# A selective-scan block on one core: projections in neighbouring slots, C products in the other two of four, one read per job

## What is computed

```python
xz = h @ in_w                       # xs and z, 512 channels each
xs = silu(xs)
proj = xs @ xproj_w                 # dt (512), B (64), C (64)
dt = softplus(proj[..., :512] + dt_bias)
A = -exp(A_log)
# at each time step, for 512 channels x 64 states:
hst = hst * exp(dt_t[:, :, None] * A) + (dt_t * x_t)[:, :, None] * B_t[:, None, :]
y_t = einsum('bds,bs->bd', hst, C_t)
# after the scan
y = (ys + xs * Dskip) * silu(z) @ out_w
```

## Time and profile before

| | us |
|---|---|
| median of 3 runs (5270.68 to 5274.25) | 5272.7 |
| the profiled execution's own time | 5272.58 |
| its span | 5270.9 |
| PE busy | 4869.9 (92%) |
| DVE busy | 4721.3 (90%) |
| POOL busy | 3754.7 (71%) |
| ACT busy | 3384.6 (64%) |
| DVE scans (L894), 2048 of them | 4536.0 |

### The profile page before, as it was taken

How to read it: one execution, slowest core, us unless ns; L and a number is a source line. 1 busy time by engine, 2 the same in 40 slices (tenths; PEclk the granted TensorE clock), 3 DMA queues, 4 the chain that set the end, 5 groups by cost and what they waited for, 6 DMA issues and landing times. The chain is left out here.

```text
span 5270.9 us, 130492 instructions
## 1 busy us (share of the span) xinstructions
PE 4869.9 (92%) x44784; PEld 2658.3 (50%) x44784; DVE 4721.3 (90%) x2419; ACT 3384.6 (64%) x11498; POOL 3754.7 (71%) x6613
## 2 busy tenths in 40 slices
PE   6999999999999999999999999999999999776898
PEld 4555555555555555555555555555555555443444
DVE  2999999999999999999999999999999999996443
ACT  4767767676766766676766767676676767663112
POOL 4787878777787878777787878687887878674211
PEclk8999999999999999999999999999999999998999
DMA  3121211112121211112121211111121211113442
GB/s 107 39 65 45 65 38 54 56 39 62 43 61 44 66 41 50 56 40 62 43 61 43 67 40 52 55 45 56 43 61 43 64 40 46 31 29 111 145 153 68
DMA packets 433144, 306.75 MB, mean 58 GB/s; under 512 B 215920, under 2 KB 336240, under 8 KB 432496
## 3 DMA queue, kind: packets, MB, share of 16 engines
q1 hardware_dynamic: 428272, 294.39, 18.7%
q10 hardware_dynamic: 4224, 4.19, 0.2%
HBM read 187.27 MB, written 111.15 MB: 57 GB/s over the span
## 5 line engine op out<-in xcount | busy, mean ns | idle before, releaser
L894 DVE TENSOR_TENSOR_SCAN b_hs<-b_dA,b_u 128x1024 f32<-128x1024 f32 x2048 | 4536.0, 2270 | 184.5 <-ACT b_u L821 155.5
L1057 PE MATMUL b_ex<-b_dd,b_aw 32*128 32x512 f32 x8192 | 2751.5, 641 | 17.6 <-POOL b_dd L542 15.6
L1044 PE MATMUL b_u<-b_ud,b_bw 32*128 32x256 f32 x16384 | 2320.1, 400 | 276.9 <-DVE b_hs L894 255.9
L803 ACT ACTIVATE b_dA<-b_ex 128x496 f32<-128x496 f32 x4096 | 2303.5, 593 | 166.0 <-PE b_ex L1057 127.5
L1044 PEld LDWEIGHTS b_u<-b_ud,b_bw 32*128 32x128 f32 x16384 | 1417.5, 184 | 1122.7 <-issue 558.1
L821 ACT ACTIVATE b_u<-b_hin 128x32 f32<-128x32 f32 x1792 | 368.8, 206 | 1236.8 <-PE b_u L1044 1045.4
L542 POOL TENSOR_TENSOR b_dd<-b_dr,b_mask 128x512 f32<-128x512 f32 x1024 | 1074.9, 1050 | 51.5 <-DVE b_hs L894 39.8
L1076 PE MATMUL b_y<-b_hs,b_cw 128*32 128x256 f32 x16384 | 1104.8, 385 | 1.7 <-DVE b_hs L894 1.7
L551 POOL TENSOR_TENSOR b_ud<-b_ur,b_mask 128x512 f32<-128x512 f32 x1024 | 1085.6, 1060 | 0.0
L1057 PEld LDWEIGHTS b_ex<-b_dd,b_aw 32*128 32x128 f32 x8192 | 865.4, 183 | 62.0 <-ACT b_dA L803 35.7
L1076 PEld LDWEIGHTS b_y<-b_hs,b_cw 128*32 128x32 f32 x16384 | 426.9, 108 | 846.2 <-issue 663.3
(11 more groups left out here) (104 smaller groups left out, 2351.0 us busy)
## 6 DMA issues: line engine op xcount, KB each, us to landing
b_u<-scratch_ut SPq DMA_DIRECT2D x256, 128.0 KB, 2.9
scratch_y<-b_ysb SPq DMA_DIRECT2D x128, 256.0 KB, 2.1
scratch_xs<-b_xs SPq DMA_DIRECT2D x64, 256.0 KB, 2.5
scratch_sz<-b_sd SPq DMA_DIRECT2D x64, 256.0 KB, 2.2
scratch_dt<-b_sd SPq DMA_DIRECT2D x64, 256.0 KB, 2.1
scratch_ut<-b_uT SPq DMA_DIRECT2D x64, 256.0 KB, 2.6
b_ur<-scratch_ut SPq DMA_DIRECT2D x1024, 16.0 KB
b_dr<-scratch_dt SPq DMA_DIRECT2D x1024, 16.0 KB, 1.7
```

What stands on the lines that cost most here:

```text
L803: nc.scalar.activation(dA[:, j % NDA, h, :, 1:TC], src[:, :, 1:TC], ACT.Exp).then_inc(exp_done, 1)
L894: nc.vector.tensor_tensor_scan(hs[:, v, :, :, kp].rearrange("p d t -> p (d t)"), dA[:, j % NDA, :, :, :].rearrange("p h d t -> p (h d t)") ...
L1044: ins = nc.tensor.matmul(dst[:, :, tb, :], bw[row(r), c % 2, tb, :], ud[row(r), j // 2 % NPR, tb, :, :], start=(tb == 0), stop=(tb == NTB ...
L1057: nc.tensor.matmul(e[bank_of[what]][:, :], aw[row(r), p % DIRS, v, :, :].rearrange("p b s -> p (b s)"), dd[row(r), (p * PAIRS + j // 2) % ...
```

## The change

Four things move at once.

1. On PE, of every four slots the first two may have a piece of a job and the last two a C pair (before: pieces in even slots, C pairs in odd ones). The two pieces of a job, or two XZ jobs, stand in neighbouring slots. Most jobs begin a few slots earlier.
2. ACT reads a job once. `take_xz` copies; a new `bend` makes the tanh of both halves from SBUF. `take_dt` adds the bias; Abs and Relu follow from SBUF in `log_part`. The side work on ACT is two generators: `readers` is stepped between the two halves of `decay`, `works` at the slot's end, where `unit` was.
3. `share_banks` guesses anew when a holder is read: first the half 0, then the job, then the half 1.
4. `log_part` begins two slots earlier against POOL; POOL's `times_sigmoid` come one slot later for the first five, and the last three move to other slots.

```diff
-        XZ_SLOT = ((0, 2), (4, 6), (8, 10), (12, 14), (16, 18), (86, 88), (98, 100), (104, 106))
-        DT_SLOT, DT_SPAN = (22, 38, 54, 70), 3
-        BC_SLOT, BC_SPAN = (32, 48), 3
-        UT_SLOT, UT_SPAN = (64, 80, 82, 96), (2, 2, 1, 1)
-        BT_SLOT = 66
+        XZ_SLOT = ((0, 1), (4, 5), (8, 9), (12, 13), (16, 17), (84, 85), (92, 93), (100, 101))
+        DT_SLOT, DT_SPAN = (20, 36, 52, 68), 2
+        BC_SLOT, BC_SPAN = (28, 44), 2
+        UT_SLOT = (60, 76, 80, 96)
+        BT_SLOT = 61
...
-                        give(("e", 2 * (slot + 2) + h), slot + 0.9 + 0.25 * h)
+                        give(("e", 2 * (slot + 2) + h), slot + 0.9 + 0.5 * h)
...
-                        give(("job", n), slot + slots + 0.2)
+                        give(("job", n), slot + slots + 0.1)
...
+                    pool.wait_ge(relued, m + 1)
                     nc.gpsimd.tensor_tensor(sd[:, j, :], pre[:, m % 2, :], ln[:, :], ALU.add).then_inc(dt_made, 1)
...
+                    yield
                     for i in range(JB + 1):
                         yield
                         times_sigmoid(q, i)
                         yield from wait_steps(3)
-                    yield from wait_steps(9)
+                    yield from wait_steps(8)
...
                         sum_dt(q, j)
-                        yield from wait_steps(4)
+                        yield from wait_steps(2)
+                        if j + 1 == JB:
+                            times_sigmoid(q, JB + 1)
+                        yield from wait_steps(2)
                         times_x(q, j)
-                        yield from wait_steps(4 if j + 1 < JB else 2)
-                    times_sigmoid(q, JB + 1)
-                    yield from wait_steps(7)
+                        if j + 1 < JB:
+                            yield from wait_steps(4)
+                    yield from wait_steps(5)
                     times_sigmoid(q, JB + 2)
-                    yield from wait_steps(6)
+                    yield from wait_steps(8)
                     times_sigmoid(q, JB + 3)
...
-                    nc.scalar.activation(dst[:, cols], job_bank(n)[:, 0:SEQ], ACT.Copy, scale=0.5)
+                    nc.scalar.activation(dst[:, b * SEQ:(b + 1) * SEQ], job_bank(n)[:, 0:SEQ], ACT.Copy, scale=0.5
+                                         ).then_inc(freed, 1)
+
+                def bend(q, i):
+                    m = q * SILUS + i
+                    src = xs[:, i, :] if i < JB else sd[:, i - JB, :]
+                    act.wait_ge(freed, first_job(q) + XZ_JOB[i] + CB)
                     if m >= 2:
                         act.wait_ge(silu_made, m - 1)
-                    nc.scalar.activation(th[:, i % 2, cols], job_bank(n)[:, 0:SEQ], ACT.Tanh, scale=0.5).then_inc(freed, 1)
+                    nc.scalar.activation(th[:, i % 2, :], src, ACT.Tanh).then_inc(bent_up, 1)
...
+                    nc.scalar.activation(pre[:, m % 2, b * SEQ:(b + 1) * SEQ], job_bank(n)[:, 0:SEQ], ACT.Identity,
+                                         bias=dtb[:, q % DIRS, j:j + 1]).then_inc(freed, 1)
+
+                def log_part(q, j):
+
+                    m = q * JB + j
+                    act.wait_ge(freed, first_job(q) + DT_JOB[j] + CB)
                     if m:
                         act.wait_ge(nd_made, 2 * m)
-                    if m >= 2:
-                        act.wait_ge(dt_made, m - 1)
-                    nc.scalar.activation(pre[:, m % 2, cols], job_bank(n)[:, 0:SEQ], ACT.Relu, bias=bias)
-                    nc.scalar.activation(ey[:, cols], job_bank(n)[:, 0:SEQ], ACT.Abs, bias=bias).then_inc(freed, 1)
...
+                    nc.scalar.activation(ey[:, :], pre[:, m % 2, :], ACT.Abs).then_inc(bent, 1)
+                    yield
+                    act.wait_ge(bent, 3 * m + 1)
                     nc.scalar.activation(ey[:, :], ey[:, :], ACT.Exp, scale=-1.0).then_inc(bent, 1)
...
                     nc.scalar.activation(wy[:, :], wy[:, :], ACT.Identity, bias=less[:, :]).then_inc(logged, 1)
+                    yield
+                    nc.scalar.activation(pre[:, m % 2, :], pre[:, m % 2, :], ACT.Relu).then_inc(relued, 1)
...
+                def works(q):
+
+                    nc.scalar.preload_act_table_set("exp_and_others")
+                    yield from wait_steps(2)
+                    for i in range(JB + 1):
+                        bend(q, i)
+                        yield
+                        plus_one(q, i)
+                        yield from wait_steps(3)
+                    nc.scalar.preload_act_table_set("natural_log_exp_and_others")
+                    yield from wait_steps(4)
+                    for j in range(JB):
+                        yield from log_part(q, j)
...
+                    nc.scalar.preload_act_table_set("exp_and_others")
+                    yield from wait_steps(4)
+                    for i in range(JB + 1, SILUS):
+                        bend(q, i)
+                        yield
+                        plus_one(q, i)
+                        yield from wait_steps(7)
...
-                        if j + 2 < JP:
-                            decay(p, j + 2)
-                        elif not last:
-                            decay(p + 1, j + 2 - JP)
+                        if then:
+                            decay(*then, 0)
+                        next(reads, None)
+                        if then:
+                            decay(*then, 1)
                         if j % HALF == 0 and half >= 2:
                             read_y(half - 2)
-                        next(side, None)
...
+                        next(work, None)
...
-                        for b in range(CB):
-                            project_xz(q, i, b)
-                            yield from wait_steps(2)
-                    yield from wait_steps(2)
+                        project_xz(q, i, 0)
+                        yield
+                        project_xz(q, i, 1)
+                        yield from wait_steps(3)
...
-                    if k % 2 and half:
-                        add_up(half - 1, k % HALF - 1)
-                        add_up(half - 1, k % HALF)
+                    if k % 4 >= 2 and half:
+                        n = k % HALF // 4 * 2 + k % 4 - 2
+                        add_up(half - 1, 2 * n)
+                        add_up(half - 1, 2 * n + 1)
```

More of the change, by code:

```diff
@@ L775, in unit @@
-                    if norm_next:
-                        for k in range(MB):
-                            yield from modulate(c, k)
-                            yield from wait_steps(2)
+                        yield from wait_steps(3)
+                    nc.scalar.preload_act_table_set("natural_log_exp_and_others")
+                    yield from wait_steps(4)
+                    for j in range(JB):
+                        yield from log_part(q, j)
+                        if q % DIRS == 1 and q + 1 < PASSES and j == 1:
+                            yield from wait_steps(7)
+                            root(q // DIRS + 1)
+                            yield from wait_steps(4)
+                        elif j + 1 < JB:
+                            yield from wait_steps(11)
+                        else:
+                            yield from wait_steps(3)
@@ L786, in _ @@
                         pass
-                for _ in unit(0):
-                    pass
+                reads, work = readers(0), works(0)
+                for _ in range(JP):
+                    next(reads, None)
+                    next(work, None)
                 act.wait_ge(a_loaded, 16 * RT * DIRS * CB)
@@ L821, in put_carry, with one_pass @@
                     nc.scalar.activation(u[:, j % 2, :, 0:H:TC], hin[:, j % NM, :, :], ACT.Copy).then_inc(carried, 1)
[L823 removed]
+                def one_pass(p, last, reads, work):
                     for j in range(JP):
                         half = (p * JP + j) // HALF
+                        then = (p, j + 2) if j + 2 < JP else None if last else (p + 1, j + 2 - JP)
                         if j >= STEPS:
                             put_carry(p, j)
[L828 to L831 removed]
+                        if then:
+                            decay(*then, 0)
+                        next(reads, None)
+                        if then:
+                            decay(*then, 1)
                         if j % HALF == 0 and half >= 2:
                             read_y(half - 2)
[L834 to L837 removed]
+                        next(work, None)
+                for j in range(2):
+                    for h in range(2):
+                        decay(0, j, h)
                 for p in range(PASSES):
[L839 removed]
+                    more = p + 1 < PASSES
+                    one_pass(p, not more, readers(p + 1) if more else wait_steps(0), works(p + 1) if more else wait_steps(0))
                 read_y(HALVES - 2)
```

126 lines of the change are left out of this document (57 added, 69 removed).

## The result

| | before | after |
|---|---|---|
| median, us | 5272.1 (5270.7 to 5274.3) | 5343.8 (5341.0 to 5348.3) |
| span of the profiled execution | 5270.9 | 5342.7 |
| main phase | 4709.97 | 4786.31 |

The change is slower: a ratio of 1.0136, 95% interval 1.0119 to 1.0154, 72 us. The forecast was 5257 with a range to 5305.

What follows compares the result with a forecast made beforehand. DVE's scans were the floor, with 248.5 us lost to side work in fifteen passes. The new losses, 109.4 plain plus 123.9 turned, made 233.3: 15.2 gained from 5272.58, so 5257, range 5210 to 5305.

Steps and rivals of the forecast that it cites:

- the floor of 2.178: Time in us of one slot in pass 15 before the change, DVE's scans end to end; losses were counted above it.
- Pass 15 and all slots without a job: Pass 15 has no side work and was taken at 278.84 us; no loss was counted there or in slots without jobs.
- The turned blocks: In seven passes, the half 1 exponent waits for modulate; two blocks lose 2.05 and 2.0, together 4.0 us a pass.
- The sum of waits on PE: Slot losses in a pass, with small ACT and POOL terms: 13.67 us without turned blocks, 17.7 with them.
- Slots 0 to 31: Five XZ groups, two DT, one BC and a table load, less slack of .42: 6.62 us lost a pass.
- the three lone XZ groups: Three XZ groups standing alone in a pass, each losing .82 less slack of .42: 1.20 us together.
- POOL at nothing: POOL's wait for the logarithm ahead of difference was costed at nothing, since log_part starts earlier and its input is due in time.
- rival D: POOL still stands before the logarithm; only about 3 us a pass come back: 5302 us, chance .06.
- the first 16 slots of a plain pass: Sign that the forecast is right: these slots, in passes without turned blocks, get slower; the stretch with the logarithm gets faster.
- Rival B: ACT is not there when the piece is full, so its reads start late and delay PE: 5315 us, chance .25.
- C: Waits behind reads do not bind, because PE's queue runs ahead of DVE: 38 us lost, 5062 us, chance .07.
- E: A table switch also empties ACT, another 1.28 us at three places in a pass: 5315 us, chance .02.

Runs made afterwards that it cites:

- run 2: The changed kernel, with each exponent in pass 15 computed twice in the two slots of every four that have no C pair: 5333.9 us, ratio 1.0116.
- run 3: The changed kernel, with C pairs in the second and fourth slot of groups whose second slot has no job: 5314.8 us, ratio 1.0080.
- Run 7: The changed kernel, with PE given extra C products between the two exponents of slot 117 in seven turned passes: 5321.4 us, ratio 1.0090.
- run 4: The changed kernel, with turned blocks' banks held one slot longer and C pairs apart in quiet groups: 5264.0 us, ratio 0.9986.
- run 10: The kernel before, with only POOL's difference, correction, sum_dt and times_x later by two slots (the last times_x one): 5239.0 us, ratio 0.9938.
- run 11: The kernel before, with only the table loads moved, from slot 28 to 26 and from 86 to 84: 5264.0 us, ratio 0.9980.

## Why the prediction was wrong

The step that failed is that PE was priced by its waits alone. Every slot was costed from the floor of 2.178 at the full clock of the earlier trace rows, as though the new order kept it, and the lulls that this order makes (two light slots in a row, a stall of 3 us) were costed at their own length or at nothing. The runs showed that the clock falls at these lulls. None of the rivals had this. Point by point:

- **Pass 15 and all slots without a job were costed at nothing.** Pass 15 takes 14.5 us more (293.31 against 278.84). Runs 2 and 3 show the cause: the clock, through the C pairs standing together.
- **The turned blocks: mechanism right, size off.** The exponent was expected 3.6 behind the inject and starts at 3.26. The 4.0 us a pass were to be the stall; slots 112 to 119 lost 8.8 in the mean of the passes that have them. Run 7 shows that the lower clock behind the stall makes up the rest: 1.52 with it gone at the second block, for which the forecast had 2.0.
- **The sum of waits on PE: right within 1.1 us a pass.** It gave 13.67 for a plain pass, 292.5; run 4 has 293.59 in pass 7, at a clock of 1.00. Slots 0 to 31 were to lose 6.62 and lose 6.50 in the mean. The C pair of a DT group's third slot was to start .67 + 1.05 behind the inject; in run 4 it starts 1.69 behind. Most of the missing 1.1 lies in the three lone XZ groups and the transposes near slots 77 to 101.
- **POOL at nothing: right** (202.5 us of waits on the logarithm before, 9.1 after), and so rival D fell. As foretold, the first 16 slots of a plain pass are slower (1.3 lost before, 3.2 in run 4) and the stretch with the logarithm, slots 32 to 83, is faster (8.2 before, 6.1 in run 4).
- **Rival B fell.** ACT does not come late to the pieces: it stands idle before them. The time of 5343.8 lies beyond B's 5315, but for another cause. C fell, since the waits bind even at full clock (14.8 us lost in a plain pass of run 4). E fell: ACT stands idle .3 us in all ahead of sixteen loads, and in pass 7 at most .06 behind one. The reads of DT and the loads before the logarithm in the changed kernel (busy, mean ns, idle time before):

```profile
L684 ACT ACTIVATE b_pre<-b_ex,b_dtb 128x256 f32<-128x256 f32 x125 | 59.1, 473 | 80.0 <-PE b_ex L992 80.0
...
L791 ACT ACT_TABLE_LOAD x16 | 20.5, 1283 | 0.3
```

The account closes: eight plain passes 295.7 against 292.5, 25.6 us; seven turned ones 303.9 against 296.5, 51.8; pass 15, 14.5; the prologue 4.5 shorter (102.40 against 106.91). Together 87.4, and 5343.8 is 86.8 over the forecast. Of the 25.6, 1.1 a pass are missing waits, and the rest goes with the low stretches of these passes, which run 3 took away.

That run 4 then comes to 5264.0, near the forecast of 5257, is in part luck: its mend took away the stall of the turned blocks, which the forecast had priced at 4.0 us in each of seven passes, and these passes still last 296.9 against its 296.5.

## What to carry to other kernels

When work is moved between slots of an engine whose clock depends on what it does, read the gaps that the move leaves, not only the sums: the same products gathered two by two cost 14.5 us in a pass that nothing else disturbed, and products that nobody needed won 7 to 10 back. Test each part of a mixed change alone on the old kernel; here POOL's two slots and two table loads were worth 0.9%, and the reordering around them cost more than that. A mend may look small alone because another fault takes its place: runs 10 and 11 gained 32 and 7 us, together 48.

## What was not expected of the hardware

- A stall of PE can be paid twice: with the same start of the exponent, 3.26 and 3.27 behind the inject, the two slots lost 4.76 or 1.52 us, by whether PE was idle or busy while it waited.
- The granted clock fell in a pass whose PE was busy for four fifths of the time (231.34 of 293.31), and stayed up at 211.99 of 278.84 with the same products spread evenly. The larger share is itself the lower clock's, since the same rows last longer at it. So the share of busy time gave no warning, nor did PE's idle time (58.7 us of waits for the scan against 59.2 in the kernel before); the order decided.
